# Moving the next sequence's turn and first projection units into the last FFN tile of a two-layer block kernel

## The reference, cut to what matters

```python
    x = _layernorm(x + _L0_ffn_ref(x, ...), axis=-1)     # rows of the layer before, per token
    x = _layernorm(x + _L1_attn_ref(x, ...), axis=-1)    # z + proj(softmax(q k / 4) v) over 16 heads of 16
    x = _layernorm(x + _L1_ffn_ref(x, ...), axis=-1)     # gate, up, down, each input quantized to FP4 in blocks of 16
```

## Time and profile before

| | us |
|---|---|
| median of 3 runs | 1815.46 |
| lowest and highest | 1814.65, 1816.88 |
| the profiled execution's own time | 1812.12 |
| its span | 1810.6 |
| PE busy, share of the span | 90% |
| DVE busy | 70% |
| ACT busy | 46% |
| mean granted TensorE clock, of full speed | 0.948 |

### The profile page before, as it was taken

The page is one execution under the profiler, slowest core; times in us unless marked ns, Lnnn a source line. Parts: engine busy times, 40 slices in busy tenths (PEclk is TensorE's granted clock), DMA queues, the critical chain, the costliest instruction groups (busy, mean ns, idle before and its releaser), DMA issues.

```text
span 1810.6 us, 30829 instructions
## 1 busy us (share of the span) xinstructions
PE 1628.5 (90%) x10370; PEld 972.4 (54%) x10370; DVE 1276.1 (70%) x2551; ACT 838.1 (46%) x1255; POOL 251.3 (14%) x255
## 2 busy tenths in 40 slices
PE   5978999996699998889999978989997989999895
PEld 2757888885343336655433556543345654333564
DVE  3672322211589996968999688789978868997686
ACT  1302233331337784242677624257772343778412
POOL 0143222222200120200003030100203010000020
PEclk8988999998789999998999989999998998999998
DMA  3128877774312310004222000412300031220000
GB/s 130 50 71 218 271 220 235 227 228 146 61 31 37 72 37 1 1 6 90 34 40 72 2 1 1 93 21 37 76 15 1 1 65 33 37 34 2 1 1 24
DMA packets 80205, 123.39 MB, mean 68 GB/s; under 512 B 13529, under 2 KB 55770, under 8 KB 80042
## 3 DMA queue, kind: packets, MB, share of 16 engines
q1 hardware_dynamic: 70666, 93.46, 20.1%
q0 software_dynamic: 9376, 27.80, 5.3%
HBM read 76.84 MB, written 18.61 MB: 53 GB/s over the span
## 4 chain that ended last, share of the span: by engine, by line
PE 68%; DVE 16%; issue 6%; ACT 4%; SPq 3%; POOL 1%; DMA 1%; DVEq 0%; ACTq 0%; POOLq 0%
PE PS L1030 13%; PE PS L987 10%; PE PS L901 8%; PE PS L913 7%; PE PS L1145 6%; DVE MX L1517 6%; PE PS L1017 5%; PE PS L1155 5%; SPq L439 3%; PE PS L960 2%; PE PS L852 2%; PE PS L1104 1%; ACT Pb L720 1%; PE PS L1175 1%; PE PS L891 1%
## 5 line engine op out<-in xcount | busy, mean ns | idle before, releaser
L1517 DVE TENSOR_REDUCE MX<-PS 128x1 f32<-128x512 f32 x1024 | 635.7, 683 | 44.3 <-PE PS L987 41.8
L720 ACT ACTIVATE Pb<-PS 128x1024 f32<-128x1024 f32 x512 | 511.1, 1026 | 176.9 <-PE PS L1017 176.6
L987 PE MATMUL PS<-Ks,Qs 48*128 48x512 f32 x1024 | 395.8, 469 | 9.5 <-DVE MX L1517 5.4
L1017 PE MATMUL PS<-Qs,Ks 50*128 50x512 f32 x1024 | 336.0, 462 | 18.2 <-ACT Pb L720 11.6
L1030 PE MATMUL PS<-Pb,V 128*32 128x256 f32 x4096 | 315.5, 398 | 1.0
L987 PEld LDWEIGHTS PS<-Ks,Qs 48*128 48x128 f32 x1024 | 163.1, 189 | 225.7 <-DVE MX L1517 203.2
L1030 PEld LDWEIGHTS PS<-Pb,V 128*32 128x32 f32 x4096 | 91.6, 110 | 161.8 <-ACT Pb L720 84.9
L1413 DVE TENSOR_TENSOR V<-PS,V 128x512 f32<-128x512 f32 x39 | 27.0, 691 | 203.9 <-PE PS L913 203.9
L1017 PEld LDWEIGHTS PS<-Qs,Ks 50*128 50x128 f32 x1024 | 134.8, 190 | 54.4 <-ACT Pb L720 37.9
L913 PE MATMUL PS<-Pb,OT 128*128 128x256 f32 x624 | 141.0, 379 | 0.0
L643 ACT ACTIVATE OT<-PS,b1t 128x256 f32<-128x256 f32 x156 | 65.5, 471 | 158.8 <-PE PS L901 158.8
(11 more groups left out here) (286 smaller groups left out, 1897.9 us busy)
## 6 DMA issues: line engine op xcount, KB each, us to landing
Pb<-W SPq DMA_DIRECT2D x78, 512.0 KB, 4.0
y_slot<-V SPq DMA_DIRECT2D x39, 256.0 KB, 3.8
Qs<-Qh SPq DMA_DIRECT2D x128, 64.0 KB, 2.3
Ks<-Kh SPq DMA_DIRECT2D x120, 64.0 KB, 2.4
V<-b SPq DMA_DIRECT2D x39, 128.0 KB, 3.6
XT<-x_mid POOLq DMA_DIRECT2D x4, 1024.0 KB, 6.5
out<-Pb POOLq DMA_DIRECT2D x4, 1024.0 KB, 6.9
OT<-xT SPq DMA_DIRECT2D x2, 1024.0 KB, 6.3
```

Of the source, the lines that this page charges most:

```text
L720: F["ex"].inc(act.activation(Pb[:, kt % 2, 2 * qh:2 * qh + 2, :], PS[:, 2 * qh:2 * qh + 2, :], ACT.Exp, scale=0.25))
L987: F["slp"].inc(pe.matmul(PS[:, slot_bank(i), :], Qs[rows, p % NB, t * P:(t + 1) * P], Ks[rows, p % NB, kh * HALF:(kh + 1) * HALF], start=T ...
L1017: ins = pe.matmul(PS[:, 2 * qh + a, :], Ks[rows, p % NB, kt * P:(kt + 1) * P], Qs[rows, p % NB, qh * HALF:(qh + 1) * HALF], start=True, st ...
L1517: F["sld"].inc(dve.tensor_reduce(MX[:, p % 2, a, t, kh:kh + 1], PS[:, slot_bank(i), :], AX.X, ALU.max))
```

## The change

1. **PE, ACT and DVE tail of the FFN.** In the last tile (t = 7) PE issues the next sequence's turn ahead of `down(6)`, unit 0 ahead of the last tile's transposes, unit 1 ahead of `down(7)`, and units 2 and 3 behind it. ACT evacuates the turn at t = 6, ahead of `next_residual`, and unit 0 behind the table load, ahead of its copies of tile 7; units 1, 2 and 3 follow around `late_root`, and four rows of the last norm come last. DVE makes the low parts of units 0 and 1 behind the quantization, those of 2 and 3 inside `late_norm`; the second-last statistics come ahead of the last residual.
2. **Loops.** PE's body is written twice as the others' (three passes in the loop, one behind); each body begins with units 4 to 7. The first sequence's turn and units 0 to 3 stand ahead of the loop.
3. **The lead.** All values wait for the eighth low part; one tile comes behind every fourth maximum from the third on. `EARLY` is gone; values use banks 3 and 7 alone.
4. **SP.** `maxima_row(0)` stands ahead of `stack(3)`.
5. **Step 53 of the main part.** `turn_max(7)` stands behind both `weigh` calls of step 53 and not between its scores.

The core of the diff:

```diff
-            return (4, 7)[t] if t < EARLY else (3, 7)[t % 2]
+            return (3, 7)[t % 2]
...
-                for p in range(NB):
+                for p in range(NB - 1):
                     stack(p)
                 maxima_row(0)
+                stack(NB - 1)
...
                         act.preload_act_table_set("natural_log_exp_and_others")
+                        if more:
+                            F["xw"].wait(act, b, TT, 1)
+                            qk_evac(b, 1, (0,))
                     F["htp"].wait(act, b, t + 1)
...
+                    if more and t == TT - 2:
+                        turned(b, 1)
                     if more and t in (5, 6):
                         next_residual(halves[t - 5])
                 if more:
-                    turned(b, 1)
+                    qk_evac(b, 1, (1, 2))
                 late_root(1)
                 if more:
-                    F["xw"].wait(act, b, TT, 1)
-                    qk_evac(b, 1, (0,))
-                late_rows(1, (4, 5))
-                if more:
-                    qk_evac(b, 1, (1,))
-                late_rows(1, (6, 7))
-                if more:
-                    qk_evac(b, 1, (2,))
+                    qk_evac(b, 1, (3,))
+                late_rows(1, range(4, TT))
...
-                for t in range(EARLY):
-                    values(t)
-                F["vv"].wait(pe, b, 1)
-                maxima(3)
                 F["qkv"].wait(pe, b, 8)
-                for t in range(EARLY, TT):
-                    n = 5 * (t - EARLY)
-                    maxima(n + 3)
-                    if t > EARLY:
+                for t in range(TT):
+                    maxima(4 * t + 1)
+                    if t:
                         F["vv"].wait(pe, b, t)
                         keep_warm(2, 1)
-                    maxima(n + 5)
+                    maxima(4 * t + 3)
                     values(t)
...
-                        if qh and m == LAST:
-                            turn_max(NP - 1)
...
                         maxima(ahead + step)
+                        if m == LAST:
+                            turn_max(NP - 1)
...
                     if t + 1 < TT:
                         gate_up(t + 1)
+                    elif more:
+                        F["hh"].wait(pe, b, TT)
+                        turn(b, 1)
                     if t:
                         down(t - 1)
+                    if more and t == TT - 1:
+                        F["xt"].wait(pe, b, 4, 1)
+                        qk_unit(b, 1, 0)
                     F["hq"].wait(pe, b, t + 1)
...
+                if more:
+                    qk_unit(b, 1, 1)
                 down(TT - 1)
+                if more:
+                    for u in (2, 3):
+                        qk_unit(b, 1, u)
...
                     F["vel"].inc(dve.tensor_scalar(vl[:, :], mvl[:, :, 1], LN_EPS, None, ALU.add))
+                    qk_low(b, 1, ahead_units[0])
                     F["rsl"].wait(dve, b, 2 * i + 2)
...
+                late_statistics("dr", TT - 2)
+                if more:
+                    F["htp"].wait(dve, b, TT)
+                    qk_low(b, 1, (0, 1))
                 ffn_add(TT - 1)
-                late_statistics("dr", TT - 2)
-                late_norm(1, late_statistics("dr", TT - 1), TT // 2)
-                if more:
-                    qk_low(b, 1, (0, 1))
+                late_norm(1, late_statistics("dr", TT - 1), TT // 2, ((2,), (3,)) if more else ((), ()))
```

More of the change, by code:

```diff
@@ L791, in _ @@
             F["xw"].wait(act, 0, TT)
-            qk_evac(0, 0, (0, 1, 2))
+            qk_evac(0, 0, range(4))
             with act.Fori(0, B - 1) as b:
@@ L933, in _ @@
             pe.wait_ge(s_one, 1 + 16 * 2 * NB)
-            with pe.Fori(0, B) as b:
-                def turn(src, base, wait):
-                    for u in range(4):
-                        c, th = u // 2, u % 2
-                        for q in range(4):
-                            t = 4 * th + q
-                            if c == 0 and wait is not None:
-                                F["zn"].wait(pe, b, wait + t + 1)
-                            ins = pe.transpose(PS[:, u, q * P:(q + 1) * P], src[:, t, c * P:(c + 1) * P], ident[:, :])
-                        F["trp"].inc(ins)
-                turn(ZN, 0, 0)
-                F["xt"].wait(pe, b, 4)
-                for u in range(8):
-                    c, w, th = u // 4, (u % 4) // 2, u % 2
-                    if u >= 4:
-                        F["qkv"].wait(pe, b, u - 3)
-                    for kc in range(DC):
-                        if w:
-                            tokens = XT[:, kc, th * HALF:(th + 1) * HALF].rearrange("p (i q) -> p i q", q=P)
-                        else:
-                            tokens = XT[:, kc, :].rearrange("p (h i c q) -> p h c i q", h=2, i=2, c=2, q=P)[:, th, :, :, :]
-                        o = PS[:, u % 4, :].rearrange("p (i q) -> p i q", q=P) if w else \
-                            PS[:, u % 4, :].rearrange("p (c i q) -> p c i q", c=2, q=P)
-                        ins = pe.matmul(o, wqkv[:, kc, w * D + c * P:w * D + (c + 1) * P], tokens,
-                                        start=(kc == 0), stop=(kc == DC - 1))
-                    F["qkp"].inc(ins)
@@ new lines, in turn, with qk_unit @@
+            def turn(b, ahead):
+                for u in range(4):
+                    c, th = u // 2, u % 2
+                    for q in range(4):
+                        t = 4 * th + q
+                        if c == 0:
+                            F["zn"].wait(pe, b, t + 1, ahead)
+                        ins = pe.transpose(PS[:, u, q * P:(q + 1) * P], ZN[:, t, c * P:(c + 1) * P], ident[:, :])
+                    F["trp"].inc(ins)
+            def qk_unit(b, ahead, u):
+                c, w, th = u // 4, (u % 4) // 2, u % 2
+                if u >= 4:
+                    F["qkv"].wait(pe, b, u - 3, ahead)
+                for kc in range(DC):
+                    if w:
+                        tokens = XT[:, kc, th * HALF:(th + 1) * HALF].rearrange("p (i q) -> p i q", q=P)
+                    else:
+                        tokens = XT[:, kc, :].rearrange("p (h i c q) -> p h c i q", h=2, i=2, c=2, q=P)[:, th, :, :, :]
+                    o = PS[:, u % 4, :].rearrange("p (i q) -> p i q", q=P) if w else \
+                        PS[:, u % 4, :].rearrange("p (c i q) -> p c i q", c=2, q=P)
+                    ins = pe.matmul(o, wqkv[:, kc, w * D + c * P:w * D + (c + 1) * P], tokens,
+                                    start=(kc == 0), stop=(kc == DC - 1))
+                F["qkp"].inc(ins)
@@ L963, in values, with sequence @@
+            def sequence(b, more):
+                for u in range(4, 8):
+                    qk_unit(b, 0, u)
                 def values(t):
@@ L1178, in _ @@
                     F["htp"].inc(ins)
+                if more:
+                    qk_unit(b, 1, 1)
                 down(TT - 1)
+                if more:
+                    for u in (2, 3):
+                        qk_unit(b, 1, u)
+            turn(0, 0)
+            F["xt"].wait(pe, 0, 4)
+            for u in range(4):
+                qk_unit(0, 0, u)
+            with pe.Fori(0, B - 1) as b:
+                sequence(b, True)
+            sequence(B - 1, False)
         @block.vector
@@ L1507, in late_norm @@
                                                       ALU.subtract, ALU.mult))
-                qk_low(b, 0, range(2, 8))
+                qk_low(b, 0, range(4, 8))
                 def row_maxima(lo, hi):
```

10 lines of the change are left out of this document (4 added, 6 removed).

## The result

The changed kernel takes 1797.8 us (median of four runs, 1794.4 to 1800.2) where the kernel before, run beside it, takes 1815.9 us (1814.7 to 1816.9, four runs). The ratio is 0.989, with a 95% interval from 0.987 to 0.992: 1.1% faster, 18.1 us. The forecast was 1792.5, the range 1785 to 1800.

The account below looks back on a forecast made before the run. PE was taken as the bound (68% of the chain), with DVE bounding the leads. Boundaries -24.4, lead +2.4, step 53 -0.6 and end -0.3 took 1812.1 to 1789.2; plus 3.3 for the median, 1792.5 us, range 1785 to 1800.

Parts of the forecast that it names:

- The boundaries: Last tile's transposes to the next sequence's first reduction: 18.35 us each, gains of 8.7, 7.8 and 7.9, in sum 24.4.
- The jump: Rival: PE's stall at the loop's branch shows between units 3 and 4 in two boundaries, +6.4 us, 1799; chance 10%.
- Unit 0: Rival: projection unit 0 starts late behind ACT's copies and the transposes slip, +5 us, 1798; chance 6%.
- The lead PE-bound: Rival: a lead group takes 2.65 us on PE, so four leads cost +8 us, 1800; chance 10%.
- The lead: First reduction to first transposed scores: 25.0 us in all four sequences, a cost of 2.4 us.
- slower: Rival: PE's new idle of about 1.8 us drops the clock through each lead, 12 us a lead, 1840; chance 4%.
- the sign that I had named for being wrong: In the lead: a granted clock of 0.50 was listed among the observations that would show the forecast wrong.
- The transpose at step 53: Main part: weighting goes ahead of the transpose that waited 1.0 us over four for DVE; gain 0.6 us.
- The end: Very end of the program: one row of statistics leaves it, once; gain between 0 and 0.6, taken as 0.3 us.
- The sum: Whole kernel: -24.4 + 2.4 - 0.6 - 0.3 = -22.9 us against the profiled 1812.1 us.

Follow-up runs that it names:

- the run with the filled FFN: Kernel before, with 22 unread identity matmuls in PE's idle stretch ahead of the last FFN tile's transposes; ratio 1.001 (0.998 to 1.005).
- the run with the fuller first group: Changed kernel with two more filler matmuls in the lead's first group, right behind PE's wait, which stays; median 1805.3 us, ratio 0.990 (0.983 to 0.996).
- the step-53 run: Changed kernel with the transpose of the last pair's maxima put back inside the unit of scores; 1795.2 us in a single run.

## Why the prediction was right, and where not

**The boundaries** (24.4 predicted) gave 25.1. The new schedule stood as written in it, each boundary 18.1 where 18.35 was worked out. Unit 0 filled the idle time, units 2 and 3 followed the last down at once, and PE waited 1.74 where I wrote 1.8.

**The jump** did not show on PE. Units 2 to 7 run without a gap at the two boundaries that cross it, and these two are as long as the third, which does not (18.14, 18.14, 18.12). The Trainium skill, "Runtime: NRT & Kernel Launch", Instruction fetch mechanics, has a taken branch out of the pages held stop execution for a fetch. The run with the filled FFN agrees that PE stalls at its jump: 0.7 to 1.1 us of idle with 3.05 us of matmuls ahead of the branch, none with 4.6 or more. In the change the last down and units 2 and 3 stand ahead of the branch, 6.4 us of matmuls, and nothing of the stall reached the path. So the rival had the stall right and the cover wrong. DVE's 3.23 us of "issue" have gone into a gap of 1.69 us that ended with ACT's unit. At the third boundary, without the jump, that gap is 0.68 us and ACT's unit comes 0.74 us earlier against the first reduction, so ACT and DVE come some 0.7 us later where they cross the jump, and that was slack.

**Unit 0** was not late: it ran 794.50 to 796.4, its copies done before. **The lead PE-bound** at the full clock did not come either, a group being 2.30 against DVE's 2.40.

**The lead** is the step that failed: I wrote "+1.5, +0.2, -0.8 and +1.5: a cost of 2.4", and it is +8.0. Its working at the full clock was good: a group 2.30 us against my 2.33, the eighth tile at 16.2 against 16.4, the transpose at 21.0 against 21.5, the scores 24.4 against 25.0. Four leads of 24.4 would have cost +0.3. The other 7.7 us are the low clock in three of four leads. That is the mechanism of my rival **slower**, to which I gave 4%. Its price was right, a group of 3.69 for my 3.5, and 10.6 to 11.8 us for my 12 in a lead nearly wholly at the low clock, but I took it as all or nothing. The clock fell in most leads of the change and came back after 3 to 10 us on the chip of the result, after 17 to 31 on the other in the second to fourth, where it took back the whole gain. Its factor of 1.57 mixed two levels: the clock was back at 1.00 from 801.90 on, inside the row of 4.79 us. A tile of values wholly at the lower level takes 2.07 us for 1.13, a factor of 1.83. I had argued against the rival that a wait of 1.57 us ahead of the first unit left the units at full pace. That row was no evidence: the run with the old order behind the wait shows that what follows the wait matters.

So the sign that I had named for being wrong, a clock of 0.50 within the lead, did appear, and that the time still lies within the range is in part luck. It hung on low stretches of 3 to 10 us; with one of 34 us, as in the run with the fuller first group on a like chip, a single lead loses 13.7.

What the runs show of the cause, counted over all leads:

- wait and new order, with the new boundary ahead (the change on both chips, the step-53 run, the fuller first group): low in 12 of 12 leads behind a boundary;
- wait and new order, without it (the first lead of each of these four runs, and all four of the new lead alone): low in 1 of 8;
- wait filled, or old order, with the new boundary ahead (six runs, the one with both changes to SP and lead among them): low in 0 of 18 leads behind a boundary, and in none of their six first leads.

So three things are needed in nearly every case: the idle time, the new order behind it and the new boundary ahead. That the order counts while the wait stays rests on one run, three leads behind a boundary. Of the boundary I can only say what else differs: the eight leads without it had seen the low level 13 to 21 us earlier, at the tail of the FFN or in the program's first part, the twelve with it not for 74 us or more. That this is the reason was not tried, and it stays open. The Trainium skill, "TensorE: Matmul & The Clock Gate", A second HAM failure mode: psum-queue depth-cycling, tells of a kernel whose short idle times between groups of matmuls let the clock swing between its two levels. The leads of the change show such a swing behind a single wait, 0.52 and 0.97 in two neighbouring windows, but by the run with the old order behind a wait of 1.56 us, and by the one with the new lead alone behind 1.74 us, idle time alone does not bring it about.

**The transpose at step 53** (0.6) took 1.2 us of idle time from ACT, which nearly bounds these steps. PE's own wait at line 994 was 0.24 each, and ACT gained 0.30 from it, where I took 0.15. No run separates it in the whole time. **The end** (0.3) can't be told apart: the stretches from scores to the next boundary, and to the end, sum to -0.5 with those 1.2 in them.

**The sum.** -25.1 + 8.0 - 0.6 = -17.7, against -22.9 predicted, and the medians of both kernels stand 3.3 to 3.8 above their profiled executions. The forecast was 5.3 us too low: the lead was 5.6 over its 2.4, the boundaries 0.7 better than worked out, and step 53 with the end 0.3 short of their 0.9.

**A better version** is the change without its lead: the turn and the units within the FFN, the values in their old order, the rows ahead of stack 3. On the slower chip it gave 0.979 (0.975 to 0.984) beside 1.000 (0.996 to 1.004) for the change. On the other chip its twin with SP's old order gave 0.982 (0.978 to 0.987) beside the 0.989 (0.987 to 0.992) of the result, and the SP edit would be worth another 1.8 us in the leads.

## What to carry to other kernels

When an edit takes fill-in work out of a wait on TensorE, price the clock as well as the wait: a wait of 1.7 us was followed by leads up to 14 us longer. Seven unread matmuls in the wait, or two tiles of useful work placed there, kept the clock up in every lead. Look at the granted clock over the stretch behind each new wait before believing in the sum of the parts. And where an edit has several parts, run the best one alone: here the lead's new order lost 0.9 us a lead with the clock held and more without.

## What was not expected of the hardware

The kernel before takes 1815 us on one chip and 1865 on another, from the same program. The clock is at its lower level for 116 us behind the first lead in the one profile and for 219 in the other. A window of the kernel before on the slower chip:

```profile
630.00:660.00 30.00, 29.09 (x189) 9.62 (x189) 20.45 (x35) 16.49 (x17) 7.09 (x8) 0.66 0.12 34
```

and the same window on the other:

```profile
630.00:660.00 30.00, 29.91 (x277) 11.25 (x277) 29.00 (x50) 23.82 (x25) 10.41 (x11) 1.00 0.17 49
```

PE is busy to 29 or 30 of 30 us in both, at 0.66 and at 1.00. The low stretches behind the first lead last longer there too, up to 23.9 us in the kernel before against 14.0 on the other chip. PE is busy all through them: in the run with the new lead alone one lasts 51.2 us with PE busy in all 51.2. Whether it is the chip, its surroundings or the phase of the program was not tried. The change was worth 18 us on one chip and none on the other, and what each part does had to be read by comparing parts of the profiles.
